# Expert stage of a small language-model tower: three banks for the third products, four places for Silu rows, the experts of a pair summed on VectorE

## The reference

```
flat = _rmsnorm(x, ln2_w).reshape(-1, Cx)
probs = jax.nn.softmax(flat @ router_w.T, axis=-1)
tp, ti = jax.lax.top_k(probs, TOPK)
tp = tp / (jnp.sum(tp, axis=-1, keepdims=True) + 1e-09)
weights = jnp.sum(tp[..., None] * jax.nn.one_hot(ti, NE), axis=1)
for e in range(NE):
    hh = jax.nn.silu(flat @ w1[e].T) * (flat @ w3[e].T)
    out = out + weights[:, e:e + 1] * (hh @ w2[e].T)
return x + out.reshape(Bx, Tx, Cx)
```

## Time and profile before

| what | us |
|---|---|
| runs of the kernel (3) | 244.35, 245.43, 245.56 |
| median | 245.43 |
| profiled execution, whole | 245.12 |
| its span, first to last instruction | 243.3 |
| TensorE matmul busy | 206.2 (85%) |
| TensorE weight load busy | 134.7 (55%) |
| VectorE busy | 178.8 (73%) |
| ScalarE busy | 153.6 (63%) |
| GpSimd busy | 144.1 (59%) |

### The profile page before, as it was taken

How to read it: one execution, slowest core, us unless ns; L and a number is a source line. 1 busy time by engine, 2 the same in 40 slices (tenths; PEclk the granted TensorE clock), 3 DMA queues, 4 the chain that set the end, 5 groups by cost and what they waited for, 6 DMA issues and landing times.

```text
span 243.3 us, 7308 instructions
## 1 busy us (share of the span) xinstructions
PE 206.2 (85%) x2828; PEld 134.7 (55%) x2836; DVE 178.8 (73%) x417; ACT 153.6 (63%) x277; POOL 144.1 (59%) x196
## 2 busy tenths in 40 slices
PE   7987788888897997976888979988899899888991
PEld 3654446445554755655666757644465465465671
DVE  4224665959878599979975879569868964999586
ACT  2368867277794677876356556577675579576670
POOL 6840000133677657574568896737989784777771
PEclk9999999999999999999999999999999999999998
DMA  2577300000000000000000000000000000010010
GB/s 43 118 164 176 83 5 3 0 3 3 3 1 3 3 3 3 3 3 0 3 3 0 3 0 3 4 0 1 3 3 1 3 23 3 0 24 0 3 24 22
DMA packets 8396, 4.51 MB, mean 19 GB/s; under 512 B 7556, under 2 KB 7852, under 8 KB 8364
## 3 DMA queue, kind: packets, MB, share of 16 engines
q1 hardware_dynamic: 8364, 4.06, 7.3%
HBM read 3.53 MB, written 0.52 MB: 17 GB/s over the span
## 4 chain that ended last, share of the span: by engine, by line
PE 41%; DVE 29%; ACT 12%; issue 10%; POOL 6%; DVEq 0%; POOLq 0%; ACTq 0%
PE bank L1369 39%; DVE shared L1330 3%; DVE nmx L1120 2%; ACT early L671 2%; ACT oTx L662 1%; ACT oT L656 1%; DVE shared L968 1%; DVE L L1297 1%; POOL shared L414 1%; DVE oT L1150 1%; ACT qT L814 1%; DVE early L861 1%; ACT early L565 1%; DVE nmr L1129 1%; DVE s L1167 1%
## 5 line engine op out<-in xcount | busy, mean ns | idle before, releaser
L1369 PE MATMUL bank<-early 64*64 64x256 f32 (+5 forms) x556 | 56.5, 352 | 10.8 <-DVE early L861 2.7
L414 POOL TENSOR_TENSOR shared<-shared 128x512 f16<-128x512 f32 x44 | 51.3, 1166 | 17.1 <-ACT shared L799 14.4
L1369 PEld LDWEIGHTS bank<-early 64*64 64x64 f32 (+3 forms) x556 | 30.7, 126 | 28.4 <-issue 5.2
L1330 DVE SCALAR_TENSOR_TENSOR shared<-bank,qT 128x512 f32<-128x512 f32 x44 | 29.7, 687 | 12.4 <-ACT qT L814 11.5
L799 ACT CAST shared<-shared 128x512 f16<-128x512 f32 x44 | 27.0, 614 | 12.1 <-DVE shared L1330 12.1
L814 ACT ACTIVATE qT<-bank 128x512 f32<-128x512 f32 x44 | 26.3, 597 | 10.5 <-PE bank L1369 10.3
L349 POOL TENSOR_TENSOR stat<-stat,neghalf 128x4 f32<-128x4 f32 x8 | 8.2, 1021 | 37.0 <-DVE stat L946 35.7
L1369 PE MATMUL bank<-onehot,w3h 128*128 128x512 f16 x88 | 26.3, 380 | 3.7 <-DVE shared L1330 3.5
L1369 PE MATMUL bank<-onehot,w1h 128*128 128x512 f16 x88 | 26.2, 379 | 0.3 <-ACT qT L814 0.3
L481 POOL TENSOR_TENSOR oTx<-oT,oTx 128x512 f16<-128x512 f32 x16 | 18.5, 1159 | 13.0 <-ACT oTx L662 12.9
L1369 PE MATMUL bank<-w2xh,shared 128*128 128x128 f16 (+1 forms) x240 | 22.4, 209 | 2.8 <-POOL shared L414 2.4
(11 more groups left out here) (228 smaller groups left out, 460.2 us busy)
## 6 DMA issues: line engine op xcount, KB each, us to landing
early<-in_tcn_w_dram SPq DMA_DIRECT2D x2, 320.0 KB, 4.2
w1s<-in_w1m_dram SPq DMA_DIRECT2D x2, 256.0 KB, 3.6
qT<-in_w3m_dram SPq DMA_DIRECT2D x2, 256.0 KB, 3.8
out_dram<-L SPq DMA_DIRECT2D x8, 64.0 KB, 1.7
qw<-in_attn_q_dram SPq DMA_DIRECT2D x4, 64.0 KB, 2.5
hTs<-in_w2m_dram SPq DMA_DIRECT2D x1, 256.0 KB
cos<-in_cos_t_dram SPq DMA_DIRECT2D x2, 96.0 KB, 2.5
sin<-in_sin_t_dram SPq DMA_DIRECT2D x2, 96.0 KB, 2.4
```

The costliest lines, as they stand in the source:

```text
L414: nc.gpsimd.tensor_tensor(hhx[:, i, 1, :], hh[:, u % RING, :], hhx[:, i, 0, :], ALU.subtract).then_inc(S["lo_ready"], 1)
L1330: V_.scalar_tensor_tensor(hh[:, u % RING, :], bank[B_BANK[u % 2]][:, :], HH_SCALE / FFN_SCALE, sil[:, u % 2, :], ALU.mult, ALU.mult).then_ ...
L1369: return nc.tensor.matmul(out_, l_, r_, start=a, stop=z, skip_group_check=skip)
```

## The change

- The third products of units 0 to 3 stay in banks 3 and 5. From unit 4 on they rotate over banks 7, 3 and 5, and wait for h(u - 3), not for h(u - 2). Unit 4 waits until bank 7 has been read by the attention's last step (`ym_ready`). The scratch place of the ranks moves from bank 7 to bank 2.
- The Silu rows have four places. The Silu of unit u waits for h(u - 4), not for h(u - 2).
- `sum_up` is gone from TensorE. VectorE keeps one running sum per group: `first_mix` (one instruction), `second_mix` and `third_mix` (a product in PSUM, then an addition into `moe`), `fourth_mix` (the same, its sum left in bank 1) and `result`, which now takes two instructions.
- The down products of k = 0 and k = 1 move from i = 5, 6, 8, 9 to i = 6, 7, 9, 10 for groups 0 to 2, and k = 2 moves wholly to i = 0, 1 of the next group (two of its four tiles were at i = 10), k = 3 to i = 3, 4. In group 3, k = 0, 1 and 2 begin at i = 5, 8 and 10. `down(n_, 1, ...)` now waits for the result of the group before, since that is read from bank 1.

```diff
-        sil = qT[:, :, 3, :]
+        sil = [qT[:, 0, 3, :], qT[:, 1, 3, :], qT[:, 0, 0, :], qT[:, 0, 1, :]]
...
+        def third_bank(u):
+
+            return bank[(3, 5)[u % 2] if u < 4 else (7, 3, 5)[(u - 4) % 3]]
...
                 act.wait_ge(S["a_ps"], u + 1)
-                if u >= 2:
-                    act.wait_ge(S["hh_ready"], u - 1)
-                nc.scalar.activation(sil[:, u % 2, :], bank[A_BANK[u % 2]][:, :], ACT.Silu,
+                if u >= 4:
+                    act.wait_ge(S["hh_ready"], u - 3)
+                nc.scalar.activation(sil[u % 4], bank[A_BANK[u % 2]][:, :], ACT.Silu,
...
+            def second_mix(n_):
+                d_, w_ = weigh(n_, 1)
+                link(V_.tensor_tensor(d_, d_, w_, ALU.mult))
+                dve.wait_ge(S["mix_ready"], 2 * n_ + 1)
+                V_.tensor_tensor(moe[:, :, :, :], d_, moe[:, :, :, :], ALU.add).then_inc(S["added"], 1)
...
+            def fourth_mix(n_):
+                d_, w_ = weigh(n_, 3)
+                link(V_.tensor_tensor(d_, d_, w_, ALU.mult))
+                dve.wait_ge(S["mix_ready"], 2 * n_ + 2)
+                V_.tensor_tensor(d_, d_, moe[:, :, :, :], ALU.add).then_inc(S["odd_mixed"], 1)
...
+                dve.wait_ge(S["odd_mixed"], n_ + 1)
                 dve.wait_ge(S["hx_ready"], n_ + 1)
-                dve.wait_ge(S["sum_ps"], 2 * n_ + 2)
-                V_.tensor_tensor(fin[:, g4, :], bank[SUM_BANK][:, 0:256].rearrange("p (t c) -> p t c", c=C),
-                                 hx[:, g4, :], ALU.add).then_inc(S["fin_ready"], 2)
+                link(V_.tensor_tensor(fin[:, g4, :], d_[:, :, 0, :], hx[:, g4, :], ALU.add))
+                V_.tensor_tensor(fin[:, g4, :], d_[:, :, 1, :], fin[:, g4, :], ALU.add).then_inc(S["fin_ready"], 2)
...
-                if n_ and i == 1:
-                    mix(n_ - 1, 2, DOWN_BANK[0])
-                if n_ and i == 4:
-                    mix_add(n_ - 1, 3)
-                if n_ and i == 8:
-                    result(n_ - 1)
-                if i == 7:
-                    mix(n_, 0, DOWN_BANK[0])
-                if i == 10 and n_ < PAIRS - 1:
-                    mix_add(n_, 1)
+                if n_ and i == 0:
+                    second_mix(n_ - 1)
+                if n_ and i == 2:
+                    third_mix(n_ - 1)
+                if n_ and i == 5:
+                    fourth_mix(n_ - 1)
+                if n_ and i == 6:
+                    result(n_ - 1)
+                if i == (8 if n_ < PAIRS - 1 else 7):
+                    first_mix(n_)
...
-                if v >= 2:
-                    pe.wait_ge(S["added" if k % 2 else "mix_ready"], v // 2)
+                if v >= 2 and k != 1:
+                    pe.wait_ge(S["added"] if k == 3 else S["mix_ready"], n_ + 1 if k == 3 else v // 2)
+                if n_ and k == 1:
+                    pe.wait_ge(S["fin_ready"], 2 * n_)
...
-            def sum_up(n_, k):
...
+                if n_ and i in (0, 1):
+                    down(n_ - 1, 2, 2 * i)
+                    down(n_ - 1, 2, 2 * i + 1)
+                if n_ and i in (3, 4):
+                    down(n_ - 1, 3, 2 * i - 6)
+                    down(n_ - 1, 3, 2 * i - 5)
+                for k, first in enumerate((6, 9) if n_ < PAIRS - 1 else (5, 8, 10)):
+                    if i in (first, first + 1):
+                        down(n_, k, 2 * (i - first))
+                        down(n_, k, 2 * (i - first) + 1)
```

More of the change, by code:

```diff
@@ L181, in tower @@
                  "rexp_ready", "gate_ready", "a_ps", "b_ps", "sil_ready", "hh_ready", "w2_ps", "mix_ready",
[L182 removed]
+                 "added", "odd_mixed", "last_acc", "last_odd", "fin_ready", "wts_ready", "w1cast", "w2_scaled", "w2_cast", "hx_ready", "hi_ready", "lo_ready",
                  "wt_zero_low", "wt_zero_high"]
@@ L200, in tower @@
         ROUTE_BANK = ((1, 0), (1, 0), (2, 256), (2, 288))
[L201 to L204, removed]
+        A_BANK, DOWN_BANK, ROW_BANK, LAST_BANK = (0, 4), (6, 1), 2, (0, 2)
+        geP = bank[2][:, 0:256].rearrange("p (a i j) -> p a i j", a=4, j=NE)
+        lP = bank[2][:, 320:352].rearrange("p (a e) -> p a e", a=4)
+        sumP, recP = bank[2][:, 352:356], bank[2][:, 356:360]
+        def third_bank(u):
+            return bank[(3, 5)[u % 2] if u < 4 else (7, 3, 5)[(u - 4) % 3]]
         def stack_bank(g):
@@ L1252, in downs, with weigh @@
                 return bank[b_][:, :].rearrange("p (t e c) -> p t e c", t=4, e=2)[:, tt, :, :]
[L1254 to L1263, removed]
-                dve.wait_ge(S["w2_ps"], 16 * n_ + 4 * k + 4)
[L1265 to L1268, removed]
+            def weigh(n_, k):
+                d_ = downs(DOWN_BANK[k % 2], slice(0, 4))
+                dve.wait_ge(S["w2_ps"], 16 * n_ + 4 * k + 4)
+                return d_, weights_of(n_, k, slice(0, 4))
@@ new lines, in first_mix, with third_mix @@
+            def first_mix(n_):
+                d_, w_ = weigh(n_, 0)
+                V_.tensor_tensor(moe[:, :, :, :], d_, w_, ALU.mult).then_inc(S["mix_ready"], 1)
+            def second_mix(n_):
[3 more added lines that the diff above has]
+                V_.tensor_tensor(moe[:, :, :, :], d_, moe[:, :, :, :], ALU.add).then_inc(S["added"], 1)
+            def third_mix(n_):
+                d_, w_ = weigh(n_, 2)
+                link(V_.tensor_tensor(d_, d_, w_, ALU.mult))
+                dve.wait_ge(S["added"], n_ + 1)
+                V_.tensor_tensor(moe[:, :, :, :], d_, moe[:, :, :, :], ALU.add).then_inc(S["mix_ready"], 1)
@@ L1913, in _ @@
                     pe.wait_ge(S["fTs_ready"], n_ + 1)
[L1914 to L1924, removed]
+                if u == 0:
+                    pe.wait_ge(S["wlow_ready"], 2)
+                    pe.wait_ge(S["nmT_ready"], B)
+                if u >= 2:
+                    pe.wait_ge(S["sil_ready"], u - 1)
+                for w in range(2):
+                    r = mm(bank[A_BANK[u % 2]][:, :], w1h[:, w, ORDER[i], :], rhs, w == 0, w == 1)
+                r.then_inc(S["a_ps"], 1)
+                if u == 0:
+                    pe.wait_ge(S["max_ready"], 3 * B)
+                if u == 1:
+                    pe.wait_ge(S["exp2_ready"], 3 * B - 1)
+                if u in (2, 3):
+                    pe.wait_ge(S["hh_ready"], u - 1)
+                if u == 4:
+                    pe.wait_ge(S["ym_ready"], TILES)
+                if u >= 5:
+                    pe.wait_ge(S["hh_ready"], u - 2)
+                for w in range(2):
+                    r = mm(third_bank(u)[:, :], w3h[:, w, ORDER[i], :], rhs, w == 0, w == 1)
+                r.then_inc(S["b_ps"], 1)
                 if u == 0:
@@ L1929, in _ @@
                 if u == 10:
[L1930 removed]
+                    f_transposed(2, ROW_BANK)
                 if u == 12:
[L1932 removed]
+                    routed(2, ROW_BANK)
                 if u == 20:
[L1934 removed]
+                    f_transposed(3, ROW_BANK)
                 if u == 22:
[L1936 to L1945, removed]
[L1946 to L1963 removed]
+                    routed(3, ROW_BANK)
+                if n_ and i in (0, 1):
[8 more added lines that the diff above has]
+                        down(n_, k, 2 * (i - first) + 1)
             down(PAIRS - 1, 2, 2)
```

46 lines of the change are left out of this document (14 added, 32 removed).

## The result

The changed kernel is slower. Its runs took 250.52, 247.73, 247.84 and 247.95 us, median 247.89, against a median of 245.23 for the kernel before (four runs, the three shown and one more beside it). The ratio is 1.0138, with a 95% interval of 1.0108 to 1.0168. I had forecast 245.2, no change, in a range up to 247.1; the time lies above it. Seven more runs of the same kernel, taken later, took 245.64 to 248.10, median 247.87, ratio 1.0084 [1.0048, 1.012].

A forecast was written before the change was run, and what follows sets the result against it. The stage was taken as two VectorE-bound stretches alternating with two where TensorE is full. Followed between meeting points, delays were mostly absorbed: 245.12 - 0.1 = 245.0, stated as 245.2 for rounding and small steps; range 242.9 to 247.1.

The forecast's parts named there:

- Up to h(13): Stage start to h(13): unchanged, held by GpSimd's split and `rms_square(3)`'s wait; TensorE arrives earlier and waits about 2 us.
- h(13) to h(20): VectorE's queue from 184.37 to h(20) at 197.0, against 195.43 before: 1.6 us later.
- h(20) to h(24): ScalarE's cast and Silu chain sets the pace, TensorE being ahead; 1.6 us made good, h(24) at 204.5, 0.35 before the old.
- The value of the third bank: Third products on TensorE: removes up to 8.4 us of waits but feeds VectorE no sooner; counted 0 alone, at most 3.8 us.
- h(24) to h(43): VectorE's queue makes h(36) 1.5 us later; then `down(3, 1)` waits for the result; unit 43's first product at 233.9, against 234.01.
- The Silu places: Silu's looser wait in four places gains nothing, since ScalarE's order already puts the cast of h(u - 2) first; both bounds 0.
- Faster rival: TensorE is the bound, so removed `sum_up` returns its whole time in TensorE's full stretches: 242.3 to 243.3, say 243.0; chance 0.27.
- the first of the two stretches: 195.5 to 205.8, where TensorE is busy 9.88 of 10.30 us; the other is 224.6 to 235.3.
- Slower rival: `down(3, 1)`'s wait passes on VectorE's delay, priced by a slower ScalarE chain before h(24): 246.4, or 247.3; chance 0.29.

The follow-up runs named there:

- again: Second profile of the changed kernel, with no edit, from a 247.87 us run (span 245.6).
- the two runs whose clock leaves no room for a fall: Two of the seven later runs of the unedited changed kernel, mean granted clock 0.995: 245.70 and 245.64 us.
- repeated products: Changed kernel with TensorE repeating the first product of unit 20 five times and of unit 31 four times; median 245.77 us, ratio 1.0052.
- gates later: Changed kernel with the gates of groups 1 and 2 one unit later; median 248.04 us, ratio 1.0135.
- fourth earlier: Changed kernel with `fourth_mix` one unit earlier, at i = 4 instead of 5; median 246.50 us, ratio 1.006.
- two Silu places: Changed kernel with two Silu places and Silu's old wait for h(u - 2); median 248.35 us, ratio 1.0133.
- the last run: Kernel before the change, only the ranks' scratch place moved from PSUM bank 7 to SBUF; median 255.44 us, ratio 1.0413.

## Why the prediction was wrong, point by point

*Up to h(13): right.* 22.57 us from h(0), 22.59 before. The prediction's remark that VectorE "never rests" in 180.8 to 195.5 was too strong: of the 1.38 us missing there, 0.52 and 0.26 are waits for GpSimd and ScalarE; the sum does not use it. GpSimd's split and `head_sum` hold h(13), and TensorE rests behind unit 10 for about 2 us, as said. I costed that rest at nothing; in some executions of the variants it is where the clock falls.

*h(13) to h(20): 0.5 us too short,* 13.13 us against 12.63. `rms_rows(3)` was taken at 0.34 from the trace before; it took 0.89, since the pile put it beside a running GpSimd instruction. With the fourth mix one unit earlier it is back to 0.33.

*h(20) to h(24): this is the step that failed.* The prediction said: "now TensorE is ahead (no `sum_up`, no wait for h) and the cast and Silu chain sets it", which "made good" the 1.6 us. It took 9.33 us in "again", not 7.5. TensorE was ahead, ran dry, and worked at half clock just when it was needed. With TensorE kept busy the step takes 7.71, so its arithmetic was right and its assumption, a granted clock of 1.00 all through, was not: it foresaw longer waits of TensorE and put their cost at nothing. The whole stretch from h(13) is 20.84 then: the 20.13 forecast, the 0.5 of the rows, and 0.2.

*The value of the third bank: wrong.* I wrote that it feeds VectorE no sooner. In the old order, with the scratch place in SBUF, nothing speaks against it: the traces with and without the bank are level up to h(19). In the new one it is worth 1.2 us in the traces at a held clock, since it is what lets TensorE have the products ready after the pile.

*h(24) to h(43): right.* 30.70 us against 30.7. To h(36) it is 21.69, 21.85 said, and from there 9.01, 8.8 said, so a little of the agreement is luck. `down(3, 1)` waits for VectorE's result, for 0.61 us, and from its start (233.92) to the first product of unit 43 (236.18) it takes 2.26, 2.27 said. The removal of two VectorE instructions shows that the stretch up to h(36) is VectorE's.

*The Silu places: right,* shown by the run with two.

*Faster rival: refuted as a main case.* Half the `sum_up` gives 0.85 us, and nothing of it in the first of the two stretches.

*Slower rival: right in sign, wrong in mechanism.* I priced a slower ScalarE chain. It was TensorE's clock. The forecast without a fall, corrected for the rows, is 245.7, and so are the two runs whose clock leaves no room for a fall. Of the 2.2 us between them and "again", 1.6 are the fall at 196. The fall at 216 adds nothing up to h(43). Another 0.5 lies outside the span (2.27 us around it in "again", 1.80 and 1.74 in those two runs), where no trace shows what it is; the prediction had put 1.82 there.

That the falls cost the time is shown by three things: the same program at two times with two clocks, the runs with more TensorE work and less time, and the half-speed matmuls in the trace, with ScalarE waiting for them. The Trainium skill ("TensorE: Matmul & The Clock Gate", What's actually happening) says that recent activity sets the gate, that the two states are 1.2 and 2.4 GHz, and that the time of a change varies from run to run; the granted 0.50 and 1.00 here and the two times of one program agree. What rest makes it fall stays open. A wait of 2.38 us was followed by a fall and one of 2.39 us was not. The same wait of 2.01 us behind unit 10 was followed by one in three traces (repeated products, gates later, fourth earlier) and not in three others (both of the changed kernel, two Silu places). Filling one rest can bring a fall at another.

## What to carry to other kernels

Work taken from TensorE is not free time when another engine is full: look at where TensorE would then run dry, and ask what its next stretch costs at half clock. An engine whose waits "cost nothing" can still set the pace afterwards. Spread long pieces of VectorE work between the products that feed the others, and check on several executions, since one program can have two times.

## What the runs showed of the hardware

- A granted clock of 0.50 lasted 3.4 us ("again", 196.2 to 199.6), though TensorE was busy without a gap in it. A pair of 512-column matmuls took 0.83 us from start to start (196.71 to 197.54), not 0.43.
- Small VectorE instructions with both inputs in SBUF that began while a GpSimd instruction ran lasted until it had ended. In the last run one started at 187.35 and took 1.26 us, until 188.61, while GpSimd's ran from 186.96 to 188.34; the same one with an input in PSUM takes 0.43. It is not the place alone: with both inputs in SBUF, one that began at 186.90, ahead of GpSimd's, took 0.42. In "again" `rms_rows(3)`, which took 0.97 us beside a GpSimd instruction (191.41 to 192.57) and 0.41 with GpSimd idle in "fourth earlier", behaves alike. A copy from SBUF to SBUF was stretched too (L1198, 1.10 us at 223.08 beside a GpSimd instruction from 222.99; the copy into PSUM takes 0.18). Over the four groups that cost 9 to 10 us of 245, more than any other edit here. The Trainium skill ("GPSIMD Engine Reference", 1. Specifications) names this contention, for instructions with two SBUF inputs; the trace agrees and gives the price.
- h itself, with one input in PSUM and one in SBUF, kept its mean of 0.686 to 0.688 us in every trace, with GpSimd busy most of the stage.
